# An adaLN block on one core: batch 0's keys copied raw out of PSUM, its scale made in four blocks of columns, and the FFN's gate folded into the weights

## The reference, cut to what matters

```python
mod = (silu(c) @ wmod).reshape(4, 6, 1, -1)          # c: 4 x 1024, wmod: 1024 x 6144
sa, ca, ga, sb, cb, gb = mod ...                      # ga, gb: kept 0.25 away from zero
h = layernorm(x) * (1 + ca) + sa                      # x: 4 batches x 1024 tokens x 1024
x = x + ga * attention(h, Wqkv, bqkv, Wo, bo)         # one head of width 256
h = layernorm(x) * (1 + cb) + sb
x = x + gb * (h @ weight.T + bias + lora(h))          # 1024 x 1024, an adapter of rank 16 chosen by batch
```

## Time and profile before

| | us |
|---|---|
| median of 3 runs (lowest, highest) | 1042.85 (1041.23, 1042.93) |
| the profiled execution, its own time | 1042.57 |
| its span (first to last instruction) | 1040.8 |
| PE busy | 1011.5 (97%) |
| DVE busy | 663.6 (64%) |
| ACT busy | 309.2 (30%) |
| POOL busy | 231.2 (22%) |

### The profile page before, as it was taken

How to read it: one execution, slowest core, us unless ns; L and a number is a source line. 1 busy time by engine, 2 the same in 40 slices (tenths; PEclk the granted TensorE clock), 3 DMA queues, 4 the chain that set the end, 5 groups by cost and what they waited for, 6 DMA issues and landing times.

```text
span 1040.8 us, 12891 instructions
## 1 busy us (share of the span) xinstructions
PE 1011.5 (97%) x5158; PEld 831.6 (80%) x5158; DVE 663.6 (64%) x827; ACT 309.2 (30%) x460; POOL 231.2 (22%) x182
## 2 busy tenths in 40 slices
PE   4899999999999999999999999999999999999996
PEld 1677777888888889888898888888887888888885
DVE  4866756498744398532976548776688578566622
ACT  1422333123232132420234523322432333142300
POOL 0000000423201322004230034342223315042411
PEclk9899999999999999999999999999999999999999
DMA  9987574767102553024443146565553646463421
GB/s 348 409 317 244 211 295 140 252 227 265 70 1 77 207 197 127 1 94 157 155 162 117 41 142 225 203 220 184 200 202 126 216 145 202 140 225 122 142 76 66
DMA packets 54475, 180.74 MB, mean 174 GB/s; under 512 B 5784, under 2 KB 6352, under 8 KB 54416
## 3 DMA queue, kind: packets, MB, share of 16 engines
q1 hardware_dynamic: 45152, 146.35, 40.9%
q0 software_dynamic: 9104, 33.04, 8.4%
q10 hardware_dynamic: 160, 0.53, 0.1%
HBM read 146.25 MB, written 33.65 MB: 173 GB/s over the span
## 4 chain that ended last, share of the span: by engine, by line
PE 91%; DMA 4%; DVE 2%; SPq 1%; issue 1%; POOL 0%; ACT 0%; DVEq 0%; POOLq 0%; ACTq 0%
PE pairC L1370 8%; PE pairA L1370 8%; PE pairC L1371 8%; PE pairC L1372 7%; PE pairA L1371 7%; PE pairA L1372 7%; PE pairD L1370 7%; PE pairD L1371 7%; PE pairD L1372 7%; PE pairB L1370 5%; PE pairB L1371 5%; PE pairB L1372 5%; DMA z_cols<-in_x_cols 2%; PE pairB L1526 1%; PE pairD L1478 1%; PE pairA L1478 1%
## 5 line engine op out<-in xcount | busy, mean ns | idle before, releaser
L923 POOL TENSOR_TENSOR xr<-xr,row_bc 128x1024 f32<-128x1024 f32 x32 | 79.9, 2503 | 110.1 <-DMA xr<-in_x 90.3
L936 POOL TENSOR_TENSOR res<-res,row_bc 128x1024 f32<-128x1024 f32 x32 | 81.7, 2565 | 83.4 <-DMA res<-x_dram 76.9
L1370 PE MATMUL pairC<-w_hi,h_hi 128*128 128x512 f32 (+1 forms) x256 | 90.1, 352 | 0.0
L1371 PE MATMUL pairC<-w_lo,h_hi 128*128 128x512 f32 (+1 forms) x256 | 90.0, 351 | 0.0
L1372 PE MATMUL pairC<-w_hi,h_lo 128*128 128x512 f32 (+1 forms) x256 | 89.6, 350 | 0.0
L1370 PE MATMUL pairD<-w_hi,h_hi 128*128 128x512 f32 (+1 forms) x224 | 77.6, 346 | 0.0
L1371 PE MATMUL pairD<-w_lo,h_hi 128*128 128x512 f32 (+1 forms) x224 | 77.6, 346 | 0.0
L1372 PE MATMUL pairD<-w_hi,h_lo 128*128 128x512 f32 (+1 forms) x224 | 77.2, 345 | 0.0
L928 POOL DMA_DIRECT2D x_dram<-xr x32 | 18.0, 562 | 229.3 <-DVE xr L1276 229.3
L1079 ACT ACTIVATE w_hi<-w_sum 128x1024 fp32r<-128x1024 f32 x32 | 33.8, 1059 | 100.5 <-DVE w_sum L1320 100.2
L1370 PE MATMUL pairB<-w_hi,h_hi 128*128 128x512 f32 (+1 forms) x160 | 59.8, 374 | 0.0
(11 more groups left out here) (344 smaller groups left out, 2570.9 us busy)
## 6 DMA issues: line engine op xcount, KB each, us to landing
wm<-in_wmod SPq DMA_DIRECT2D x48, 512.0 KB, 6.4
xr<-in_x SPq DMA_DIRECT2D x34, 512.0 KB, 4.0
z_cols<-in_x_cols SPq DMA_DIRECT2D x32, 512.0 KB, 6.3
x_dram<-xr POOLq DMA_DIRECT2D x32, 512.0 KB, 3.8
xs<-x_dram SPq DMA_DIRECT2D x32, 512.0 KB, 4.7
w2t<-in_w2t SPq DMA_DIRECT2D x32, 512.0 KB, 4.3
res<-x_dram SPq DMA_DIRECT2D x32, 512.0 KB, 5.7
out_y<-res POOLq DMA_DIRECT2D x31, 512.0 KB, 3.5
```

Of the source, the lines that this page charges most:

```text
L923: nc.gpsimd.tensor_tensor(xt, xt, row_bc[:, :], ALU.add).then_inc(residual_made, 1)
L936: nc.gpsimd.tensor_tensor(rt, rt, row, ALU.add).then_inc(residual2_made, 1)
L1370: nc.tensor.matmul(out, left[0], right[0], start=first, stop=False)
L1371: nc.tensor.matmul(out, left[0], right[1], start=False, stop=False)
```

## The change

1. **The scale of batch 0 in four blocks of 256 columns.** `M(0,*)`, `MC(0)`, `MT(0)`, `MM(0)` become `M0(c)`, `MC0(c)`, `MT0(c)`, `MM0(c)`, c = 0 to 3. Each takes two DMAs of four row tiles by 256 columns, 1 KB a piece where it was 4 KB. `HH(0,0,k)` waits for block k alone. The values of the first half are made in column blocks too (`V0`), beside `K0`.
2. **The statistics of both halves of batch 0 are spread by PE** (`BCM` for the mean, which doesn't wait for 1/sigma, `BCP` for 1/sigma), and ACT copies them from PSUM to `bc` (`BMC`, `BPC`). The way through DRAM goes for this half (`RT0(0,1)`, `SC`, `SW`, `LBC`).
3. **Batch 0's keys raw.** ACT copies them out of PSUM without the bias (`KR`, four steps), and `KH`/`KL` read that copy later.
4. **wmod's tiles from the second part on use four buffers** (six and then four before).
5. **The gate goes into the weights.** `WG` multiplies `w_sum` by the gate in place, between `WS` and `WH2`, 32 steps. `FG` is gone, `FA` adds PSUM to `res` directly, and frees the pair.
6. **All five orders are written anew.**

```diff
-                eng.wait_ge(y_gated, f_no(*i) + 1)
+                eng.wait_ge(y_made, f_no(*i) + 1)
...
+                    if s == CA:
+                        half, at = k % 2, q * H + k // 2 * 2 * P
+                        src = wmod[half * BANK:(half + 1) * BANK, at:at + 2 * P].rearrange("(k p) n -> p k n", p=P)
+                        sp.dma_start(wm[k].rearrange("p (k n) -> p k n", k=4), src).then_inc(ld_wm[k], 16)
+                        return
...
+                elif what == "MC0":
+                    c = i[0]
+                    act.wait_ge(mod_used, 2 * c + 2)
+                    wait(act, ca_turned, c - 1)
+                    nc.scalar.activation(mod_rows[:, c % 2 * 2 * P:(c % 2 + 1) * 2 * P], ps[:, 0:2 * P], ACT.Copy).then_inc(ca_copied, 1)
...
+                elif what == "KR":
+                    _, j, m = i
+                    act.wait_ge(k_done, 2 * j + m + 1)
+                    act.wait_ge(mod_used, 6)
+                    nc.scalar.activation(k_raw[:, m, j * CHUNK:(j + 1) * CHUNK], ps[:, m * BANK:(m + 1) * BANK],
+                                         ACT.Copy).then_inc(k_raw_made, 1)
...
-                    act.wait_ge(w_sum_made, 8 * b + n + 1)
+                    act.wait_ge(w_gated, 8 * b + n + 1)
...
-                    if q == 0:
-                        dve.wait_ge(stat_spread, 1)
+                    if b == 0:
+                        dve.wait_ge(spread_copied, 2 * j + 2)
...
+                elif what == "WG":
+                    b, n = i
+                    h = n // 4
+                    dve.wait_ge(ld_gate2, 16 * (b + 1))
+                    dve.wait_ge(w_sum_made, 8 * b + n + 1)
+                    wt = w_sum[:, n % 2, :].rearrange("p (c n) -> p c n", c=2)
+                    gate = gate_bc[:, h * BANK:(h + 1) * BANK].unsqueeze(1).to_broadcast([P, 2, BANK])
+                    nc.vector.tensor_tensor(wt, wt, gate, ALU.mult).then_inc(w_gated, 1)
...
-                    gate = gate_bc[:, h * BANK:(h + 1) * BANK].unsqueeze(1).to_broadcast([P, 2, BANK])
-                    nc.vector.tensor_tensor(gated[:, :].rearrange("p (t n) -> p t n", t=2),
-                                            ps[:, :].rearrange("p (t n) -> p t n", t=2), gate, ALU.mult).then_inc(y_gated, 1)
...
-                    nc.vector.tensor_tensor(res[:, slot, :], res[:, slot, :], gated[:, :], ALU.add).then_inc(y_made, 1)
+                    nc.vector.tensor_tensor(res[:, slot, :], res[:, slot, :], ps[:, :], ALU.add).then_inc(y_made, 1)
```

More of the change, by code:

```diff
@@ L521, in build_block @@
             with ExitStack() as early:
-                wm = [sb(f"wm{i}", [P, H], at=early) for i in range(4)]
+                wm_pair = [sb(f"wm{i}", [P, 2, H], at=early) for i in range(2)]
             wo_hi = sb("wo_hi", [P, DT, H], F32R, at=first)
@@ L533, in build_block @@
             q_lo = sb("q_lo", [P, DT, S], F32R, at=first)
+            k_hi = sb("k_hi", [P, DT, S], F32R, at=first)
+            with ExitStack() as early:
+                wm_pair += [sb(f"wm{i}", [P, 2, H], at=early) for i in (2, 3)]
+            with ExitStack() as early:
+                k_raw = sb("k_raw", [P, DT, S], at=early)
             k_lo = sb("k_lo", [P, DT, S], F32R, at=first)
-            with ExitStack() as early:
-                wm += [sb(f"wm{i}", [P, H], at=early) for i in (4, 5, 6, 7)]
-            k_hi = sb("k_hi", [P, DT, S], F32R, at=first)
             v_hi = sb("v_hi", [P, QT, D], F32R, at=first)
             v_lo = sb("v_lo", [P, QT, D], F32R, at=first)
+        wm = [wm_pair[i // 2][:, i % 2, :] for i in range(8)]
         wo_raw = [xr, probs, probs, probs]
@@ L676, in wm_slot @@
         def wm_slot(n):
-            return n if n < 8 else (n - 8) % 6 if n < 16 else n % 4
+            return n if n < 8 else n % 4
         def wm_turn(n):
@@ L709, in wait_emptied @@
             if what == "M":
-                eng.wait_ge(mod_made, i[0] + 1)
-            elif what == "BCP":
-                eng.wait_ge(z_made, 4)
+                eng.wait_ge(mod_made, i[0])
+            elif what == "M0":
+                eng.wait_ge(ca_made, i[0] + 1)
+            elif what == "BCM":
+                eng.wait_ge(spread_copied, 2 * i[0] + 2)
             elif what == "WU":
@@ L726, in wait_emptied @@
                 eng.wait_ge(q_lo_made, 4 * i[0] + 2 * i[1] + 2)
+            elif what == "K" and i[0] == 0:
+                eng.wait_ge(k_raw_made, 2 * i[1] + 2)
             elif what == "K":
@@ L860, in step @@
                     else:
-                        sp.wait_ge(y_gated if what == "LG2" else residual2_made, 8 * b)
+                        sp.wait_ge(w_gated if what == "LG2" else residual2_made, 8 * b)
                     at = ((GB_ROW if what == "LG2" else BIAS_ROW) * B + b) * CT
@@ L961, in step @@
                     act.wait_ge(mod_used, CT * (s + 1))
-                    wait(act, mod_turned, s)
+                    if s == SA:
+                        act.wait_ge(ca_turned, 4)
+                    else:
+                        act.wait_ge(mod_turned, s - 1)
                     if s == GA:
@@ L1229, in step @@
                     dve.wait_ge(hi_made, 4 * b + 2 * j + m + 1)
-                    nc.vector.scalar_tensor_tensor(lo[where], ps[:, m * BANK:(m + 1) * BANK],
+                    src = k_raw[where] if what == "KL" and b == 0 else ps[:, m * BANK:(m + 1) * BANK]
+                    nc.vector.scalar_tensor_tensor(lo[where], src,
                                                    bias_qkv[:, col + m, b:b + 1], hi[where].bitcast(F32),
@@ L1369, in product3 @@
             def product3(out, left, right, first, last):
-                nc.tensor.matmul(out, left[0], right[0], start=first, stop=False)
-                nc.tensor.matmul(out, left[0], right[1], start=False, stop=False)
-                return nc.tensor.matmul(out, left[1], right[0], start=False, stop=last)
+                nc.tensor.matmul(out, left[0], right[0], start=first, stop=False, skip_group_check=True)
+                nc.tensor.matmul(out, left[0], right[1], start=False, stop=False, skip_group_check=True)
+                return nc.tensor.matmul(out, left[1], right[0], start=False, stop=last, skip_group_check=True)
             def both(hi, lo, *where):
@@ L1383, in step @@
                         nc.tensor.matmul(ps[:, 0:BANK], w_hi[:, 0, D:D + P], w_hi[:, 0:2, D:2 * D], start=True, stop=True)
+                elif what == "M0":
+                    c = i[0]
+                    if c == 0:
+                        pe.wait_ge(c_ready, 1)
+                    for k in range(CT):
+                        if k % 4 == 0:
+                            pe.wait_ge(ld_wm[2 * c + k // 4], 16)
+                        q = 32 * (k % 4)
+                        last = nc.tensor.matmul(ps[q:q + 32, 0:2 * P], scT[:, k * B:k * B + 32],
+                                                wm[2 * c + k // 4][:, k % 4 * 2 * P:(k % 4 + 1) * 2 * P],
+                                                start=(k < 4), stop=(k >= 4))
+                        if k % 4 == 3:
+                            last.then_inc(mod_used, 1)
+                elif what == "MT0":
+                    c = i[0]
+                    pe.wait_ge(ld_const, 16)
+                    pe.wait_ge(ca_copied, c + 1)
+                    for cc in range(2):
+                        at, col = BANK + B * cc, c % 2 * 2 * P + cc * P
+                        last = nc.tensor.matmul(ps[:, at:at + B], mod_rows[:, col:col + P], sel, start=True, stop=True)
+                    last.then_inc(ca_turned, 1)
                 elif what == "M":
                     s, r = i
-                    if s + r == 0:
-                        pe.wait_ge(c_ready, 1)
                     for k in range(2 * r, 2 * r + 2):
@@ L1405, in step @@
                     last.then_inc(mod_turned, 1)
-                elif what == "BCP":
+                elif what in ("BCM", "BCP"):
+                    j = i[0]
                     pe.wait_ge(ld_const, 16)
-                    pe.wait_ge(rstd_made, 1)
-                    for k in range(2):
-                        for t in range(4):
-                            at = k * CHUNK + t * P
-                            last = nc.tensor.matmul(ps[:, at:at + P], stat[:, 0, k, t:t + 1].to_broadcast([P, P]), ident,
-                                                    start=True, stop=True)
-                    last.then_inc(stat_spread, 1)
+                    if what == "BCM":
+                        pe.wait_ge(stat_made, 4 * j + 4)
+                    else:
+                        pe.wait_ge(rstd_made, j + 1)
+                    k = 0 if what == "BCM" else 1
+                    for t in range(4):
+                        at = k * CHUNK + t * P
+                        last = nc.tensor.matmul(ps[:, at:at + P], stat[:, j, k, t:t + 1].to_broadcast([P, P]), ident,
+                                                start=True, stop=True)
```

(13 more changed lines are left out.)

146 lines of the change are left out of this document (72 added, 74 removed), and 700 rows, old and new, of tables (ACT_ORDER, DVE_ORDER, PE_ORDER, POOL_ORDER).

## The result

The changed kernel takes 1044.03 us (median of 8 runs, 1043.36 to 1045.46), the kernel before in the same comparison 1042.28 us (8 runs, 1040.75 to 1043.67). The ratio is 1.0024, 95% interval 1.0015 to 1.0033: 1.75 us slower, where the forecast was 0.4 us faster. The profiled execution took 1044.15 us with a span of 1042.3, so 1.5 us more span than before.

A forecast was written before the change was run, and what follows sets the result against it. PE, busy 1011.5 of 1040.8 us, was taken as the bound, with DVE only 1.0 us ahead where the FFN begins. Terms -6.1 + 4.7 + 0.2 - 1.7 + 3.3 - 0.8 = -0.4 gave 1042.4 us; 8-in-10 range 1038.5 to 1045.2.

The forecast's parts named there:

- Part 5: FFN's beginning: gate products on DVE, the bound there, delay the first FFN product; plus 3.3 us, bounds 2.3 and 5.5.
- Part 4: Near 84 us: key halves between narrow steps keep PE's clock up; minus 1.7 us, bounds 0 and 1.7.
- the low clock at the first products: First key products: half clock costs the same before and after; counted 0, with 2.5 us either way.
- Part 1: Start: shorter chain brings the first key product from 30.60 to 24.5; minus 6.1 us.
- Parts 2 and 3: Work put between the key and value products, plus 4.7 us; then second half's chain, 0.2 us waiting at `SAM`.
- The four wmod buffers: wmod loads from the second part on: issued about 8 us ahead of need, so 0, bound 1 us.
- rival C: FFN's beginning: DVE and POOL collide; one gives 1043.5 to 1044.5, two about 1046.5 us; chance of two 0.17.
- Part 6: End: one DVE step behind the last matmul where there were two; minus 0.8 us.
- A: Rival: the FFN's beginning hides the gate's cost; 1038.8 us, chance 0.28.
- B: Rival: clock falls again in narrow steps between `Q(0,1,1)` and `S(0,2)`; costs 1.7 us, 1044.1 us, chance 0.10.
- own range: Whole kernel: 1040.8 to 1044.3 us, from bounds of start, second-half chain and gate taken one at a time; chance 0.45.

The follow-up runs named there:

- e9: Kernel before, plus 17 wide matmuls with unread results in PE's gaps ahead of its first key product; 1042.62 us, ratio 1.0007 to before.
- e5: Changed kernel, with POOL's bias-row addition for x1 tile (3,5) held until the first gate product is done; 1042.67 us, ratio 1.0002 to before.
- e2: Changed kernel with the gate back on the FFN's outputs, start and orders as changed; 1040.77 us, ratio 0.9990 to before.
- e4: Changed kernel with four wmod loads and one statistics load ahead of four loads of x in SP's queue; 1045.74 us, ratio 1.0047 to before.
- e10: Changed kernel plus twelve matmuls with unread results in the waits ahead of the first key product; 1041.72 us, ratio 0.9999 to before.
- e3: Changed kernel with two DVE steps exchanged, second weight sum ahead of first gate product; 1043.45 us, ratio 1.0014 to before.
- e6: Changed kernel with the gate on the outputs for batch 0's first half of columns, in the weights elsewhere; 1039.43 us, ratio 0.9970 to before.
- e1: Kernel before with only the gate moved into the weights, and gate-row and first two residual loads earlier; 1060.21 us, ratio 1.0177 to before.

## Why the prediction failed, by its own steps

Two terms failed. Part 5 put the gate at plus 3.3 us, with POOL's addition beside the first `WG` and ACT at nothing; it cost 5.0. Part 4 took off 1.7 us for a stretch at half clock that came again. A third term, the low clock at the first products, stood at 0 and cost 1.5 to 1.7 us; it didn't show in the sum, since the keys and values were done at 52.2 all the same, where 52.8 was forecast.

**Part 1 held.** First key product 24.5 forecast, 24.62 measured; `BCM` 15.0 and 14.75, `BCP` 16.9 and 17.01. The low clock at the first products was counted at 0 with 2.5 either way. It lasted 6.8 us before and 3.4 us after in the profiled executions, but before it lay under DVE (e9) and after it does not, so it is a cost of the new start that the term left at 0, as "the same before and after": 1.5 to 1.7 us, by e5's trace, which has none of it. Of the seven traces with this start and no unread matmuls e5 has none, e2 6.8 us and the other five 3.4 us.

**Parts 2 and 3 held in sum, with one bound used up.** `K0` and `V0` are done at 52.2 (forecast 52.8), `SAM` starts at 72.30 without a wait (72.8, 0.2). The four wmod buffers, counted at 0 with a bound of 1, cost 0.94 us. The step that failed there is "about 8 us ahead of need, more than the 5.7 us of the slower rows": the queue began to issue the four loads at 72.53, 9.5 us before PE wanted the first of them at 82.02, but the one shown took 10.7 us to land, behind four loads of x; with wmod ahead of them (e4) the wait was gone. In the traces with this order of loads it goes from 0 (e10) to 1.3 us (e2). Parts 1 to 3 forecast -1.2. Five executions with the new start up to the first `W` (changed, e2, e3, e5, e6) have it at 620.5 on average (619.75 to 621.62), the two with the old one (before, e1) at 622.0: -1.5, with single executions up to 1 us off, and with what part 4 counted in it.

**Part 4 failed: minus 1.7 us for a second low clock that would vanish.** It came again in the changed kernel's profiled execution (granted 0.51 at 83.8 to 87.2). But it isn't fixed to a kernel either. The same windows in e3, where every instruction up to there is the same:

```profile
80.40:83.80 3.40, 3.00 (x25) 1.71 (x25) 2.32 (x8) 1.89 (x3) 0.00 (x0) 1.00 0.97 366
83.80:87.20 3.40, 3.16 (x20) 0.89 (x13) 1.17 (x3) 1.60 (x3) 0.00 (x0) 1.00 0.99 351
```

PE does the same narrow steps, and the clock is full. Of the seven traces with the new start and its order at this place one has half clock here, of the three with the old one (before, e1, e9) one too; so whether the new order makes it rarer is open. The term took an event of one execution for a property of the order of work. Over 23 runs of the kernel before, taken beside e1 to e4, the mean granted clock of a run goes from 0.992 to 0.996, and the time with it: the five at 0.992 took 1041.6 to 1044.2 us, the two at 0.996 1040.4 and 1040.6. (That mean takes in every stretch, the one behind the last matmul too.) At best the order of work could change how often the clock falls there, and the term needed that share and took all of it.

The page TensorE: Matmul & The Clock Gate of the Trainium skill, section What's actually happening, says that the same kernel can show different numbers of slow matmuls from run to run. It says so of a kernel's first matmuls; the rows above show the same at 84 us.

**Part 5 had the right mechanism and the wrong size: plus 3.3 us forecast, plus 5.0 measured.** DVE is the bound, the waits are on `w_sum` and the last `w_lo`, and the count of steps gives 18.75 us from `W` to `F`; e3 shows 18.83 and e5 18.98. ("There it has no gap" overlooks one of 0.40 us at 631.43, for a load of `w2t`; it changes nothing here.) The 20.55 of the changed kernel hold two things more, and they are the steps that failed. POOL's addition beside the first `WG`: 1.2 us (2.41 against 1.22), which the sum had at nothing and rival C had at 1.1 to 2.1 us for one collision, "1043.5 to 1044.5". It could be seen coming: the kernel before has this addition at the same place, beside a `WS`, which it doesn't hold up.

```profile
622.73 2.38 POOL L923 TENSOR_TENSOR xr<-xr,row_bc 128x1024 f32<-128x1024 f32 x1 [1.19 <-DMA xr<-in_x]
```

And 0.6 us for ACT's `w_hi`: behind PE's wait of 2.7 us the clock fell to half, the second turn of x came 13.1 us after the first `W` (e4, with the same wait and full clock: 11.4), and with it ACT's work ahead of `w_hi` (no wait there in e4). The turn in the changed kernel and in e4:

```profile
633.72 1.03 PE L1538 MATMUL pairD<-consts,xs 128*128 128x128 f32 x8
```

```profile
632.35 1.03 PE L1538 MATMUL pairD<-consts,xs 128*128 128x128 f32 x8
```

On PE the low clock cost nothing here, since PE waited for DVE anyway; it cost through ACT. The two terms also give the other traces: 18.75 and 1.04 (the `WG` of 2.25 us) are 19.79 in e4, measured 19.77; 18.75, 1.84 and 0.68 are 21.27 in e10, measured 21.26. That the wait of DVE comes from the low clock is read from these traces; no run holds the clock alone.

**Part 6 held**, 0.8 and 0.79.

**The rivals.** A falls: the FFN's beginning does not hide the gate. B's place, 126 to 140 us, stayed at full clock. C was the right one to fear, but it was set to decide at two collisions. Its time for one, 1043.5 to 1044.5, holds the measured 1044.03, in part by luck: ahead of the first `W` 0.8 us of the forecast gain didn't come and ACT's 0.6 us came on top, and the rest of the FFN happened to be 0.65 us shorter. Its sentence that each lost us of DVE is one of PE holds at `F`: 1.2 us less in e5's step, 1.6 us less from `W` to `F`, where the 0.6 us for ACT went too and one `WL2` took 0.2 us more beside the moved addition.

**The range.** The forecast's "own range 1040.8 to 1044.3" doesn't follow from its bounds taken one at a time: keys at 27 give 1044.9, a wait of 3 us in part 3 gives 1045.2. Part 1's terms up to the low part add up to 23.4, not 23.6.

In sum, by the two profiled executions: -1.2 and -1.7 (parts 1 to 4, all ahead of the first `W`) are -2.1 together (with nothing of it from part 4), +3.3 is +5.0, -0.8 is -0.8, and -0.65 came over the rest of the FFN. That rest isn't the change: from the first `F` to PE's last matmul eleven of the twelve traces take 392.5 to 393.4 us, with the gate in either place.

## What to carry to other kernels

A stretch at half clock in one profile is a chance, not a cost of that stretch: before a change is credited with its end, look for it in several executions, and ask whether PE is the bound there at all; only then is it worth anything. When work moves ahead of a bound, count it against the engine that must do it last before the next stage, here DVE, and look for which other engine's step will overlap each moved one. And a change that wins everywhere but in one place can be cut: with the first four of 32 gate products left out of the weights, and twelve unread matmuls in the first waits, it went from 0.24% slower to 0.42% faster than the kernel before. The first step alone gave 0.30% faster; what the second adds is within the intervals.
